# Attention over sixteen images: the normalised output is transposed ahead of the last scores of a step, into the projection's bank, and the row of maxima behind the middle scores

## What is computed

```python
t = t + _L1_attn_ref(_ln_t(t), w_attn, w_proj)

def _L1_attn_ref(x, w_attn, w_proj):
    qkv = x @ w_attn
    ...
    wei = jnp.einsum('bhqd,bhkd->bhqk', q, k) * scale
    wei = jnp.where(causal[None, None], wei, -jnp.inf)
    wei = jax.nn.softmax(wei, axis=-1)
    out = jnp.einsum('bhqk,bhkd->bhqd', wei, v)
    out = out.transpose(0, 2, 1, 3).reshape(B, T, C)
    out = out @ w_proj
    return out
```

## Time and profile before

| | before |
|---|---|
| median of 3 runs | 291.05 us (289.40 to 292.52) |
| the profiled execution | 289.84 us, span 288.1 us |
| TensorE busy | 235.5 us (82%) |
| VectorE busy | 207.3 us (72%) |
| ScalarE busy | 136.7 us (47%) |
| GpSimd busy | 116.8 us (41%) |

### The profile page before, as it was taken

How to read it: one execution, slowest core, us unless ns; L and a number is a source line. 1 busy time by engine, 2 the same in 40 slices (tenths; PEclk the granted TensorE clock), 3 DMA queues, 4 the chain that set the end, 5 groups by cost and what they waited for, 6 DMA issues and landing times.

```text
span 288.1 us, 5491 instructions
## 1 busy us (share of the span) xinstructions
PE 235.5 (82%) x1880; PEld 180.0 (62%) x1880; DVE 207.3 (72%) x517; ACT 136.7 (47%) x318; POOL 116.8 (41%) x121
## 2 busy tenths in 40 slices
PE   0129899999989896588989999798998499999780
PEld 0118899888879785365877778487665245545340
DVE  0899457878898877778797676567435658898944
ACT  1331255555463434365667676457764306326420
POOL 1380404836736836445345332836427403110010
PEclk9999999999999999999999999899999689999997
DMA  4920110110029999004445544530000000101111
GB/s 123 256 49 1 27 30 0 31 27 0 31 68 120 115 122 98 3 14 99 100 100 96 98 85 89 102 60 3 4 0 3 0 0 0 41 4 40 41 40 56
DMA packets 25452, 15.66 MB, mean 54 GB/s; under 512 B 3473, under 2 KB 25298, under 8 KB 25426
## 3 DMA queue, kind: packets, MB, share of 16 engines
q1 hardware_dynamic: 23568, 14.04, 28.0%
q10 hardware_dynamic: 1858, 1.29, 2.0%
HBM read 4.26 MB, written 1.57 MB: 20 GB/s over the span
## 4 chain that ended last, share of the span: by engine, by line
PE 56%; DVE 19%; issue 11%; POOL 8%; ACT 2%; DMA 2%; DVEq 0%; SPq 0%; POOLq 0%
PE bank L1538 8%; PE bank L1552 7%; PE bank L1249 6%; PE bank L1362 6%; PE bank L1427 5%; DVE nmax L969 5%; PE bank L1365 3%; DVE xs_ring L836 3%; PE bank L1395 3%; POOL ln_rstd L433 2%; POOL parts L427 2%; PE bank L1430 2%; DMA cst<-in_const 2%; DVE qr_ring L891 2%; PE bank L1452 2%
## 5 line engine op out<-in xcount | busy, mean ns | idle before, releaser
L969 DVE TENSOR_REDUCE nmax<-bank 128x3 f32<-128x384 f32 x64 | 45.5, 751 | 23.1 <-PE bank L1365 23.0
L455 POOL TENSOR_SCALAR_AFFINE_SELECT pt_ring<-pt_ring 128x512 f32<-128x512 f32 x48 | 31.2, 651 | 51.3 <-ACT pt_ring L641 51.1
L1249 PE MATMUL bank<-xs_ring,toep 128*128 128x192 f32 x256 | 49.2, 337 | 0.6 <-issue 0.6
L641 ACT ACTIVATE pt_ring<-bank 128x384 f32<-128x384 f32 x96 | 41.9, 489 | 16.5 <-PE bank L1397 15.8
L1249 PEld LDWEIGHTS bank<-xs_ring,toep 128*128 128x128 f32 x256 | 43.3, 196 | 2.1 <-issue 0.9
L1362 PE MATMUL bank<-stack 96*128 96x128 bf16 x192 | 31.7, 250 | 4.9 <-DVE nmax L969 3.6
L427 POOL TENSOR_TENSOR parts<-rest_ring,parts 96x512 bf16<-96x512 f32 x16 | 23.6, 1476 | 23.5 <-DVE parts L868 23.5
L1365 PE MATMUL bank<-mask,ident 128*128 128x128 bf16 x192 | 31.7, 222 | 0.0
L1538 PE MATMUL bank<-parts,w_b 97*128 97x512 f32 (+1 forms) x60 | 24.4, 533 | 2.8 <-DVE parts L1116 2.8
L1362 PEld LDWEIGHTS bank<-stack 96*128 96x128 bf16 x192 | 18.6, 99 | 11.7 <-issue 6.7
L1552 PE MATMUL bank<-parts,w_b 128*96 128x512 f32 (+1 forms) x60 | 23.3, 493 | 0.9 <-issue 0.9
(11 more groups left out here) (154 smaller groups left out, 484.8 us busy)
## 6 DMA issues: line engine op xcount, KB each, us to landing
stack<-parts SPq DMA_DIRECT2D x96, 96.0 KB, 3.6
x_ring<-in_x SPq DMA_DIRECT2D x8, 192.0 KB, 2.4
out<-xs_ring SPq DMA_DIRECT2D x5, 288.0 KB, 2.6
stack<-in_x SPq DMA_DIRECT2D x2, 384.0 KB, 6.8
stack<-in_x ACTq DMA_DIRECT2D x2, 384.0 KB, 10.9
stack<-nmax_t SPq DMA_DIRECT2D x32, 1.5 KB
cst<-in_const SPq DMA_DIRECT2D x1, 384.0 KB, 11.8
w_in<-in_L_ffn_W ACTq DMA_DIRECT2D x2, 144.0 KB
```

What stands on the lines that cost most here:

```text
L455: nc.gpsimd.affine_select(out=v, in_=v, compare_op=ALU.is_ge, fill=0.0, base=0, pattern=[[0, 2], [0, 2], [1, P]], channel_multiplier=-1).t ...
L641: nc.scalar.activation(pt_ring[:, b % 2, h, :], bank[:, 3 + h % 2, 0:T + P], ACT.Exp, scale=float(HD) ** -0.5).then_inc(s_exp, 1)
L969: last = nc.vector.tensor_reduce(nmax[:, b % 2, k:k + 3], bank[:, 0:3, first:first + (t + 1) * P], op=ALU.max, axis=AX.X, negate=True)
L1249: nc.tensor.matmul(dst, w, xs_ring[:, s, p, k].rearrange("p b c -> p (b c)"), start=(k == 0 and p == 0), stop=False)
```

## The change

Three things are rearranged; no instruction is added or taken away.

- transpose_norm(n - 2, 0 and 1) stands as a pair between scores_q(n + 3, 1) and scores_k(n, 2), for all images into bank 6 (columns 0 to 255), the bank of the projection. It therefore waits for s_res. scores_k no longer waits for s_ontc.
- transpose_max(n + 2) stands behind scores_k(n, 1), no longer ahead of it.
- On ScalarE norm_out(n - 2) stands behind sums_out(n - 1), no longer ahead of values(n), and max_out(n + 2) behind exps(n, 1).

```diff
                 act.wait_ge(s_ont, b + 1)
                 wait(act, s_proj, b - 1)
-                src = bank[0:C, 3:5, 3 * P:4 * P] if b < B - 2 else bank[0:C, 6, 0:T].rearrange("c (t n) -> c t n", t=NT)
-                nc.scalar.copy(ot_ring[:, b % 2, :].rearrange("c (t n) -> c t n", t=NT), src).then_inc(s_ontc, 1)
+                nc.scalar.copy(ot_ring[:, b % 2, :], bank[0:C, 6, 0:T]).then_inc(s_ontc, 1)
...
             def step_b(n):
                 exps(n, 0)
+                exps(n, 1)
                 if n + 2 < B:
                     max_out(n + 2)
-                exps(n, 1)
-                if n >= 2:
-                    norm_out(n - 2)
                 values(n)
...
                 sums_out(n - 1)
+                if n >= 2:
+                    norm_out(n - 2)
                 exps(n, 2)
...
                 if t == 0:
                     pe.wait_ge(s_on, b + 1)
-                    if b >= B - 2:
-                        pe.wait_ge(s_res, b)
-                dst = bank[0:C, 3 + t, 3 * P:4 * P] if b < B - 2 else bank[0:C, 6, t * P:(t + 1) * P]
-                last = nc.tensor.transpose(dst, o_norm[:, t, :], ident[:])
+                    wait(pe, s_res, b)
+                last = nc.tensor.transpose(bank[0:C, 6, t * P:(t + 1) * P], o_norm[:, t, :], ident[:])
...
-                if hp == 2 and b >= 2:
-
-                    pe.wait_ge(s_ontc, b - 1)
...
-                    if hp == 1 and b >= 2:
-                        transpose_norm(b - 2, e)
...
                 scores_k(n, 0)
                 if n + 3 < B:
                     scores_q(n + 3, 0)
+                scores_k(n, 1)
                 if n + 2 < B:
                     transpose_max(n + 2)
-                scores_k(n, 1)
                 weighted_values(n - 1)
                 if n + 3 < B:
                     scores_q(n + 3, 1)
...
+                if n >= 2:
+                    for t in range(NT):
+                        transpose_norm(n - 2, t)
                 scores_k(n, 2)
```

## The result

The changed kernel takes 292.86 us (median of 22 runs, 290.53 to 295.99), the kernel before 290.91 us (22 runs, 287.75 to 293.71): ratio 1.0093, 95% interval 1.0068 to 1.0117. On another chip the same pair gave 1.0136 (1.0082 to 1.0190). The ratios leave out each kernel's runs more than 1.5% above its own fastest, here seven of the 22 before and two of the 22 after, and the medians of all runs give 1.0067. The change makes the kernel slower by about 1%, 2 to 3 us; forecast were 292.7 us and +2.1.

The account below looks back on a forecast made before the run. TensorE was taken to bound regular steps, with VectorE's maxima releasing scores_q. The terms summed to +2.1 us, 291.9 against the profiled 289.84; 292.7 was put, nearer the timed median, with 289.3 to 295.0 expected 8 times in 10.

Parts of the forecast that it names:

- What bounds the kernel: Regular loop steps: TensorE busy nearly throughout, standing 0.3 us before scores_q because VectorE's maxima release its banks late.
- First half: Regular step, first to second half of scores_q: 0.22 us shorter, 3.05 to 2.83, in seven steps, -1.54 us.
- Second half: Regular step, second half of scores_q to the next step's first: 2.64 to 2.91 us, taken as +0.26, six times, +1.56.
- Steps 2 and 3: Early loop steps: -0.65 us from a shorter wait for o_norm, +0.4 from a later transpose_o ahead of VectorE's reciprocal; together -0.25.
- Step 10: After weighted_values waits for GpSimd, at the lower clock: project_out some 0.55 us later, 0.15 filling a bubble; +0.4.
- absorption of step 9: The loss in step 9's second half vanishes, since weighted_values of step 10 waits for GpSimd until 184.36 anyway.
- Steps 12 to 15: Loop end, without scores_q to give slack: 0.23 + 0.72 + 0.39 + 0.57 us later, +1.91, carried to the end.
- the 0.5 that I had given as a sign: Expected in the profile after: TensorE idle before project_out for ot_ring 0.5 us or more in steps 13 and 15.
- Sum: Whole kernel: -1.54 + 1.56 - 0.65 + 0.4 + 0.4 + 1.91 = +2.1 us.
- That the hand-off costs nothing: Rival: ot_ring is ready when project_out comes, second halves stay 2.64 us; -2.2 us, 288.9; chance 0.13.
- That the end absorbs it: Rival: regular steps at nothing, steps 12 to 15 at 0 to +1 us, or the start gains more; 290.5 to 291.5; chance 0.22.
- That the clock falls more often: Rival: longer TensorE stops bring one or two more clock falls, 1.6 us each; 294.3 to 296 us; chance 0.15.

Follow-up runs that it names:

- old_end: The changed kernel with transpose_norm and norm_out back in their old places in steps 13, 14 and 15 only; ratio to before 1.0124.
- swap: The changed kernel with transpose_o(n - 1) ahead of project_out(n - 2) in every step; 290.27 us, ratio to before 1.0008.
- double_copy: The changed kernel with one more ScalarE copy of the same size, into a spare tile, directly ahead of the copy ot_ring; ratio to before 1.0276.
- norm_only: The changed kernel with transpose_max back ahead of scores_k(n, 1) and max_out ahead of exps(n, 1); median 294.17 us, ratio to before 1.0189.
- all_three: Changed kernel: transpose_o ahead of project_out, old transpose_norm place in steps 13 to 15, GpSimd's second-layer-norm power behind step 9's last selection; ratio to before 0.9982.
- swap_mid_late: Changed kernel: transpose_o first in steps 2 to 12, old order in 13 to 15, second layer norm's statistics, power and normalisation later; 286.94 us, ratio to before 0.9887.

## Why the prediction was right

Point by point, with the 1.1 us ahead of the loop taken off the times after.

- **What bounds the kernel.** Right. TensorE in the regular steps, with VectorE releasing Q0.
- **First half, 3.05 - 0.22 = 2.83.** Measured 2.83.
- **Second half, 2.91.** Measured 2.89. The hand-off was priced at 0.85 us and is 0.83 (180.18 to 181.01). The price came from the last image alone: of the last two, which the prediction names, image 14 has other work of TensorE in between and doesn't show it bare. In the changed kernel the bubble ahead of Q0 is gone, the one ahead of project_out is there.
- **Steps 2 and 3, -0.25.** Here the sum was too low by 0.24: the two steps together gave nothing. Step 2 gained 0.71 (135.34 before, 135.73 - 1.10 after), as forecast, and transpose_o, late by TN and the stall, made VectorE's reciprocal of step 3 0.55 later against the maxima ahead of it. But VectorE's casts to bf16 around them, which I had taken as fixed, didn't last the same: the first took 0.77 us after and 0.42 before, with one of GpSimd's selections now running beside it, and the second 1.11 after and 1.35 before. Together the casts are 0.11 of the 0.24. The rest is that I had put the late transpose_o at 0.4, as if part of it stayed hidden, where all of its 0.55 counted. The scores of step 4 start at 149.62 before and 150.71 after, with the 1.10 taken off the same: all of step 2's gain was given back by then.
- **Step 10, +0.4, and the absorption of step 9.** Right. weighted_values of step 10 is at 184.36 and at 185.62; the 1.26 us less the 1.10 is what steps 4 to 8 made of the second halves over the first (0.17, forecast 0.20), and step 9's second half left no trace. Behind it project_out comes 4.75 us after weighted_values in place of 4.21, 0.54 later (forecast 0.55), and up to the weighted_values of step 11 it is 7.33 us in place of 7.11: +0.22, where 0.4 less the 0.22 of step 11's first half was forecast.
- **Steps 12 to 15, +1.9.** From the weighted_values of step 11 to the last projection: 32.05 us before, 34.09 after, 2.04 more, of which step 11's own second half and step 12's first were forecast to leave 0.04. The terms hold one by one: up to the projection of step 13 it is 1.00 more (forecast 0.99), from there to transpose_o of step 14 another 0.50 (0.39), from there to the end 0.54 (0.57). TensorE stands 0.44 us ahead of project_out in step 13, a little under the 0.5 that I had given as a sign. old_end shows that 1.72 us of it lie behind the weighted_values of step 13.
- **Sum +2.1.** The loop's 2.42 us; on the medians 1.95. I was 0.3 short, mainly by the term of steps 2 and 3. That 292.7 and 292.86 lie so near each other is partly luck: the anchor was a median of three runs (291.05) of a kernel whose runs differ by 6 us, and the medians of 22 differ by 0.5 us less than the loops.
- **Rivals.** That the hand-off costs nothing: refuted by swap and double_copy, from both sides. That the end absorbs it: refuted by old_end's trace. That the clock falls more often: it falls in executions of either kernel, in step 10 and ahead of the loop, but the mean clock of the changed kernel's 22 runs, 0.970, is that of the kernel before beside the experiments, so the loss isn't made of it. It goes with most of the 6 us by which runs of one kernel differ (1.8 us for each 0.01 of clock, from 0.954 to 0.982). The rule of the Trainium skill cited in the prediction ("TensorE: Matmul & The Clock Gate", section "A second HAM failure mode: psum-queue depth-cycling") isn't borne out here: from 150 to 180 us the clock is at 1.00 in all nine traces whose regular steps have such a stop of TensorE (0.3 us, 0.6 in double_copy).

The recorded ratios of norm_only, old_end and double_copy, each from six runs, lie above what their loops explain; at equal clock all three agree with their loops within the interval (2.7, 1.2 and 5.6 us against 2.4, 0.7 and 6.1, low clock taken off). Of all kernels only all_three doesn't (0.7 us under before against 1.4 by its loop). The line in the clock was drawn after the fact and its intervals are wide, so for the sizes of single terms I trust the distances in the traces.

## What to carry to other kernels

When a small piece is moved into a bubble, follow its result too: here the transpositions (0.22 us) fitted into the bubble (0.3 us), but their copy comes back to the same engine 0.83 us later, and only 0.58 us of work stood between. Put an independent piece of that size between the two (transpose_o ahead of project_out), and the move pays; and look at the first and last steps of a pipeline by themselves, since the work that hides a hand-off in the middle is absent there, and the right order can be another one.

## What the runs showed of the hardware

- The clock granted to TensorE fell in some executions and not in others behind a wait of the same length: 1.47 and 1.96 us with a fall (before, changed), 1.72 and 2.05 us without (norm_only, swap), five of ten traces each way. It costs 1.3 to 1.6 us each time. Over whole runs, 0.01 of mean granted clock goes with 1.8 us of 290.
- A cast to bf16 on VectorE (96x512) took 0.42 us in the kernel before with GpSimd nearly idle, and 0.77 to 1.35 us where GpSimd worked beside it (before and changed). No run isolates GpSimd as the cause; a place on VectorE's chain is best priced with GpSimd's timeline beside it.
- SyncE needs some 0.66 us to issue each of the transfers into the stack and 0.76 for each of the row's; the eight of an image took 5.69 to 6.5 us in swap_mid_late, which is the next bound once the step is 5.49 us.
